# Two edits around the hand-over from the convolutions to the windowed attention: position-logit units one place earlier, and a mask copy made by a transfer

## The reference, cut to what matters

```
x = x + _L0_conv_ref(_gn(x), ...)                      # conv_out beside attn
k, q, v = kqv[..., :64], kqv[..., 64:128] * 8 ** -0.5, kqv[..., 128:]
rel_w = rel_logits_1d(qh, key_rel_w, H, W, (0, 1, 2, 4, 3, 5))
rel_h = rel_logits_1d(qh_t, key_rel_h, W, H, (0, 1, 4, 2, 5, 3))
weights = softmax(einsum('bnid,bnjd->bnij', qf, kf) + rel_w + rel_h)
attn = einsum('bnij,bnjd->bnid', weights, vf)
```

## Time and profile before

| | |
|---|---|
| median of 3 runs | 2134.51 us |
| the profiled execution | 2135.44 us, its span 2133.7 us |
| mean granted TensorE clock | 0.977 of full |
| PE busy | 95% of the span |
| ACT, DVE, GpSimd busy | 60%, 66%, 12% |
| convolution block | 0 to 385.7 us |
| attention block 1 | 385.9 to 452.8 us |
| attention block 2 begins | 453.2 us; period 0 lasts to about 504 us |

### The profile page before, as it was taken

The page is one execution under the profiler, slowest core; times in us unless marked ns, Lnnn a source line. Parts: engine busy times, 40 slices in busy tenths (PEclk is TensorE's granted clock), DMA queues, the critical chain, the costliest instruction groups (busy, mean ns, idle before and its releaser), DMA issues. The chain is left out here.

```text
span 2133.7 us, 27710 instructions
## 1 busy us (share of the span) xinstructions
PE 2017.6 (95%) x10112; PEld 1383.7 (65%) x10112; DVE 1405.5 (66%) x2075; ACT 1283.5 (60%) x2205; POOL 259.3 (12%) x281
## 2 busy tenths in 40 slices
PE   5999999879999999999999999999999969999997
PEld 4788888745555554454555447777777748888886
DVE  6776775657777777777777555666666545656655
ACT  4344543537777776777777656666666645556654
POOL 2000000021221212122223200000000000001000
PEclk8999999889999999999999999999999979999998
DMA  4334558885777666666677422333331154443341
GB/s 117 95 99 164 173 193 202 195 216 85 110 120 111 110 115 107 105 120 105 107 118 126 148 69 75 114 114 106 103 114 50 50 172 197 150 148 138 139 158 50
DMA packets 143030, 265.99 MB, mean 125 GB/s; under 512 B 23472, under 2 KB 87728, under 8 KB 138928
## 3 DMA queue, kind: packets, MB, share of 16 engines
q1 hardware_dynamic: 135088, 239.02, 46.6%
q0 software_dynamic: 7680, 25.17, 3.7%
q10 hardware_dynamic: 128, 0.03, 0.0%
HBM read 156.37 MB, written 107.24 MB: 124 GB/s over the span
## 5 line engine op out<-in xcount | busy, mean ns | idle before, releaser
L850 DVE TENSOR_REDUCE a_nmax<-a_sm 128x1 f32<-128x1024 f32 x512 | 603.4, 1219 | 193.0 <-PE a_sm L870 192.7
L1140 ACT ACTIVATE p_shared<-a_st 128x512 f32<-128x512 f32 x1024 | 556.7, 597 | 242.1 <-PE a_st L1168 241.0
L1183 PE MATMUL a_pv<-p_shared,a_va 128*32 128x512 f32 x2048 | 272.5, 604 | 0.0
L1168 PE MATMUL a_st<-a_qf,a_kf 121*128 121x512 f32 x704 | 251.8, 437 | 15.7 <-PEq L1207 12.8
L1168 PEld LDWEIGHTS a_st<-a_qf,a_kf 121*128 121x128 f32 x704 | 119.0, 189 | 207.7 <-ACT p_shared L1140 183.8
L870 PE MATMUL a_sm<-a_kf,a_qf 120*128 120x512 f32 x704 | 201.5, 403 | 1.9 <-PEq L250 1.8
L2163 DVE SCALAR_TENSOR_TENSOR x_h_lo<-x_hid,x_wts,x_h_hi 128x512 fp32r<-128x512 f32 x128 | 96.0, 751 | 140.6 <-ACT x_h_hi L2124 140.5
L2253 PE MATMUL x_h_ps<-x_v_hi,x_w 128*128 128x512 f32 x512 | 184.0, 401 | 0.0
L2267 PE MATMUL x_y_ps<-x_h_hi,x_w 128*128 128x512 f32 x512 | 180.7, 394 | 0.0
L2120 ACT ACTIVATE x_hid<-x_h_ps,x_bias 128x512 f32<-128x512 f32 x128 | 88.1, 688 | 140.5 <-PE x_h_ps L2253 140.5
L870 PEld LDWEIGHTS a_sm<-a_kf,a_qf 120*128 120x128 f32 x704 | 130.4, 191 | 39.4 <-issue 7.2
(11 more groups left out here) (299 smaller groups left out, 3388.4 us busy)
## 6 DMA issues: line engine op xcount, KB each, us to landing
x_w<-w_d SPq DMA_DIRECT2D x31, 1024.0 KB, 8.7
rel_d<-p_shared SPq DMA_DIRECT2D x12, 2048.0 KB, 11.5
a_qf<-rel_d SPq DMA_DIRECT2D x22, 512.0 KB
a_qf<-rel_d SPq DMA_DIRECT2D x44, 256.0 KB
c_xtok<-in_x SPq DMA_DIRECT2D x8, 1024.0 KB, 6.9
va_d<-c_va SPq DMA_DIRECT2D x16, 512.0 KB, 7.0
a_va<-va_d SPq DMA_DIRECT2D x32, 256.0 KB, 23.7
a_w_st<-in_L_ffn_W POOLq DMA_DIRECT2D x32, 256.0 KB, 9.3
```

What stands on the lines that cost most here:

```text
L850: nc.vector.tensor_reduce(nmax[:, h, t:t + 1], sm[k % 2][:], axis=AX.X, op=ALU.max, negate=True).then_inc(sm_read, 1)
L1140: nc.scalar.activation(probs[:, t % 2, h, half * HALF:(half + 1) * HALF], st[half][:], ACT.Exp).then_inc(exp_done, 1)
L1168: nc.tensor.matmul(st[half][:], kf[j][0:ROW_M + 1, h, t * P:(t + 1) * P], qf[j][0:ROW_M + 1, h, 2 * t // TT, half * HALF:(half + 1) * HALF ...
L1183: m = nc.tensor.matmul(pv[32 * h:32 * h + 32, cols], va[j][:, t, h, :], probs[:, t % 2, h, cols], start=t == 0, stop=t == TT - 1, skip_gro ...
```

## The change

It has three parts. In image 7, the eight `rel` units of set 4 stand after `v` 2 and no longer after `c0` 1. In attention block 1, SP stores set 0 first, then loads group 1's values, then stores set 1; the wait at the end is still for set 0 alone. The one-hot matrix comes into `kf[2]` no longer by four GpSimd copies at the end of block 1, but by one transfer that SP issues as the first of block 2, after a wait for set 1's store; it increments `built[2]` by 16, and SP waits for 16 before group 2's keys.

```
-            UNITS[:5] + rel(4, 0, 8) + UNITS[5:] + rel(5, 0, 8)]
+            UNITS[:4] + rel(4, 0, 8) + UNITS[4:] + rel(5, 0, 8)]
...
-                store_relative(1)
                 store_relative(0)
                 load_v(sp, 1, 1)
+                store_relative(1)
                 sp.wait_ge(rel_stored[0], 32)
 
             @block.gpsimd
             def _(pool):
                 make_identity(nc, pool, ident[:], made)
                 double_queries(pool, 1, 1)
-                pool.wait_ge(rel_stored[1], 32)
-                for h in range(HG):
-                    last = nc.gpsimd.tensor_copy(kf[BUFS - 1][:, h].rearrange("p (a n) -> p a n", a=2), group.both_halves)
-                last.then_inc(built[BUFS - 1], 1)
...
                     if isinstance(n, int) and n == BUFS - 1:
-                        sp.wait_ge(built[j], 1)
+                        sp.wait_ge(built[j], 16)
                     load_keys(sp, kq_d, n, kf[j], loaded[j])
...
                 sp.sem_inc(out_stored, 16)
+                sp.wait_ge(rel_stored[1], 32)
+                sp.dma_start(bits(kf[BUFS - 1][:]).rearrange("p h (a n) -> p (h a) n", a=2),
+                             group.ones_hot[:].rearrange("p (a n) -> p a n", a=1).to_broadcast([P, 2 * HG, HALF])).then_inc(built[BUFS - 1], 16)
                 all_groups(sp, period)
```

More of the change, by code:

```diff
@@ L955, in _ @@
                 double_queries(pool, 1, 1)
[L956 to L959, removed]
             @block.scalar
```

## The result

The changed kernel takes 2145.69 us (median of 5 runs, 2144.30 to 2147.44), the kernel before in the same session 2134.94 (2132.34 to 2135.66): ratio 1.0057, 95% interval 1.0044 to 1.0070. It is slower by 0.6%. I had forecast 2132 and at most 2139. Rival B (group 2 comes too late) names the place, but its price was 4.5 us where 10 were lost.

What follows compares the result with a forecast made beforehand. PE, busy 95%, was taken as the bound. Passing group 2's first use at 498.8 instead of 501.4 us gave −2.6: 2135.44 to 2132.8, less 0.9 for the median, forecast 2132; 8-in-10 range 2124 to 2139.

Steps and rivals of the forecast that it cites:

- Rival B: At group 2's first pass in period 0: its loads come too late, +4.5 us, 2139 us; chance 0.16.
- What bounds the kernel: PE, busy 95% of the span; convolution block's end, set 0's store landing and group 2's loading decide.
- Part 1: Image 7: set 4 earlier makes PE wait 4.5 us, the clock fall, and the convolution block end 6.7 us later.
- I take it that the clock falls here: Image 7's set 4: clock falls to 0.50 after PE's wait; its 64 matmuls take 13.7 us.
- The block ends 6.7 us later: Convolution block's end at 392.3 us against 385.66, 5.9 to 7.5 us later by the bounds on the clock.
- Rival A: Image 7: clock holds or returns within set 4, block ends about 2.0 us earlier; 2123 us, chance 0.19.
- Part 2: Block 1: set 0's store first lands at 448.7 us; PE restarts at 449.8, 4.0 us earlier than 453.83.
- That PE would restart sooner at full clock: Block 2's start: 4 us at 0.50 clock instead of 6.7, worth 1.3 us.
- Part 3: Block 2's start: after the ones, group 2 arrives at 497.8 us; PE waits 1.7 us, passes at 498.8, not 501.4.
- The 31 us for group 2's loads: Block 2: group 2's loads take 31 us, from about 455 to 486, where half the DMA engines were still busy.
- the lower bound: Block 2's transfer of ones: 2048 KB takes 5.2 us at 415 GB/s; the other bound was 10 us at 217.
- a dip of the clock: PE's wait ahead of group 2: an even chance of another clock dip, about 1 us.

Runs made afterwards that it cites:

- e3: Changed kernel plus 19 matmuls with unused results in PE's wait ahead of image 7's set 4: 2139.6 us, ratio 1.0014 to the kernel before.
- e9: The kernel before, unchanged, profiled once more: span 2133.8 us, image 7 58.88 us; no median given.
- e10: Kernel before with block 1's stores in the changed order and GpSimd's four copies moved to block 2's start: 2126.5 us, ratio 0.9959 to the kernel before.
- e1: Kernel before with only set 4 moved one unit earlier in image 7: 2139.7 us against 2137.5, ratio 1.0009.
- e8: Changed kernel with 19 matmuls ahead of set 4, GpSimd's copies in block 2 for the ones, and biases one period later: 2123.5 us, ratio 0.9939 to before.
- e6: Changed kernel with the ones copied by GpSimd at block 2's start instead of by DMA: 2130.4 us, ratio 0.9960 to the kernel before.
- e4: Changed kernel with SP's turns of the biases one period later: 2141.0 us, ratio 1.0021 to the kernel before.
- e7: Kernel before with only the DMA of ones at block 2's start in place of GpSimd's copies: 2136.2 us, ratio 0.9990 to the kernel before.
- e2: Changed kernel with image 7's unit order turned back, set 4 again after c0 1: 2141.1 us, ratio 1.0015 to the kernel before.
- e12: The e8 kernel plus 16 matmuls with unused results at block 1's end: ratio 0.9958 to the kernel before.

## Why the prediction was wrong, by its steps

**What bounds the kernel:** right. All that moved, moved at the three places named.

**Part 1.** "PE reaches set 4 and waits 4.5 us": 4.39. "I take it that the clock falls here": it was 0.50 until 357. "The block ends 6.7 us later": 5.75. Without the fall of the clock (e3) the compute ends 7.6 us sooner. Rival A, in which the clock holds, is what e3 made by hand: its "2.0 us earlier" for the end of the compute came out at 1.9, but the block's end didn't follow, since neither I nor the rival had the stores of `mixT_d`. Only my reading of the kernel before was weak: I took the wait of 3.28 us for a property of the kernel, and it varies between 3.3 and 6.8. Against e9, the middle one of five, the block ends 2.7 us later and not 5.75, so that my 6.7 came out near is owed in part to the profile that I drew.

**Part 2.** From the block's end (DVE's first instruction of block 1) to PE's first score matmul I had 56.4 us (393.4 to 449.8); the changed kernel took 57.19, before 67.17. e10 shows the gain by itself. I had set 0's store and DVE end together; the store was the last, at 450.65 by SP's wait, and DVE ended at 449.10. That PE would restart sooner at full clock I priced at 1.3 us; the clock came back at 459, against 460.5.

**Part 3 is the step that failed.** From the restart to group 2 I had 498.8 − 449.8 = 49.0 us; it took 59.97. The term is the time from the issue of the ones to the landing of the keys, 1.5 + 5.2 + 31 = 37.7; it was 511.7 − 462.6 = 49.1. The runs take it apart:
- The 31 us for group 2's loads were too few. I read them off the DMA share, between two ends that I set by eye. From SP's first issue to the keys' landing it was 34.4 in the kernel before, 36.2 in e1, 36.1 in e8 and 37.6 in e6, with no ones at all, against my 1.5 + 31 = 32.5. So the loads alone use up the 37.7 that I gave to both. Of the 5.1 us that were missing, 1.9 could have been read from the kernel before; the other 3.2 are the difference between e6 and it, whose cause wasn't looked for.
- The ones cost 6.3 us: e4, with them and with the biases out of the way, needs 506.3 − 462.4 = 43.9 us, e6 37.6. (In e7 it was 45.7, 9.5 to 11.3 more than in e1 and before; there they landed after 11.3 us instead of 9.8, why I don't know.) The stretch in which they ran:
```profile
464.00:471.00 7.00, 7.00 (x41) 3.46 (x34) 5.54 (x5) 4.78 (x9) 0.00 (x0) 1.00 1.00 292
```
  All 16 DMA engines were busy, at 292 GB/s and not at the 415 of the large stores. I chose the lower bound for a reason ("it writes all 128 partitions") that no row bore out; in the trace's packet records they go in packets of 2048 bytes, the stores in packets of 4096.
- The biases cost 5.2 us more (49.1 − 43.9). SP issues them behind the copies of the maxima, which depend on PE's first pass, so their time hardly moved: 50.8 us after PE's restart before, 51.1 now (504.60, 502.81). The keys moved from 487.7 past it. In e6 and e7 the keys land before them, and the biases cost nothing.

Together: 37.6 + 6.3 + 5.2 = 49.1. Against my 37.7 the loads are 5.1 us over, the ones 1.1 and the biases, which my sum didn't have, 5.2.

The same sum against the profile of before: the start came 2.15 us later without any part in it, image 7 −0.96 from my figure, block 1 +0.75, group 2 +10.97: 12.9 us, which is 511.71 − 498.8. (The 498.8 had in it, in full, a dip of the clock that I called an even chance.) Rival B had the right mechanism, and came to 503.4 for the arrival, since it too used the 31.

**The parts together.** By the stages, part 2 gains 10 us (e10), part 3 costs nothing alone (e7) and 12 us behind part 2 (60 against 48, e6), part 1 costs 2.3 to 5.7 (by the medians of e6 and e10 nothing that can be seen). Part 2 both brings PE earlier to group 2 and, by putting set 1's store last, sends the ones and the loads out later: before, the keys had landed 13.7 us ahead of PE (487.7, 501.41). In e7 the ones are issued 0.7 us before PE's restart, in the changed kernel 10.9 us after it (462.61, 451.74); 10.9 + 49.1 is the stage's 60.0. So part 2 used up the slack, and part 3 came to stand on the path. In e6 the keys at 499.8 are just in time for PE at 499.88.

Three things stay open. Why the clock fell in e2's block 1 and held in all others behind the same waits; what makes set 4's store land up to 3.5 us later in one execution than in the next; and where the part of the medians' loss lies that no stage shows. No run was made for any of them.

## What to carry to other kernels

Before a transfer is put on a queue ahead of loads, take the slack of the last load (landing to first use) from the records of landings, not from a picture of how busy the DMA engines are; then ask what else becomes due in the time by which the load slips. A change that wins time by an earlier restart spends that same slack, so the two are priced together. And where a wait for a transfer is a term of the sum, its length in one profile is one draw: here it went from 3.3 to 6.8 us, enough to turn a cost of 2 us into one of 6.

## What the runs showed of the hardware

- A transfer within SBUF of 2048 KB to 128 partitions, in packets of 2048 bytes, ran at about 290 GB/s with all 16 DMA engines busy, and landed 9.6 to 9.8 us after its issue (11.3 in e7); stores to DRAM of the same size in packets of 4096 bytes ran at 415.
- 3 KB of biases in elements of 4 bytes delayed the landing of 128-KB loads, issued 29 us ahead of them, by 5.2 us (e4).
- What 0.50 of the clock costs depends on what PE waits for. At the restart of block 2, where its first matmuls wait for ACT, some 5 us at 0.50 cost 1.2 us (e12 against e8). In set 4 and the unit behind it, where PE had work throughout, 17 us at 0.50 cost 7.6 us of compute (e3).
